# Gates computed with tokens on partitions, and the gated residual moved from GpSimd to VectorE

## The chip, the cores and the metric

One Trainium2 chip; the kernel runs on one of its cores. The metric is device time of one execution in microseconds (us), lower is better. PE is TensorE (PEld its weight loads), DVE is VectorE, ACT is ScalarE, POOL is GpSimd and SP is SyncE, which here issues nearly all DMAs.

## The reference

Eight batches of 512 tokens with 512 features, in f32. First a gated cross attention (an mLSTM, 4 heads of 128), then a gated mixture of 8 experts, 2 per token:

```python
ig = einsum(gin, w_igate) + b_igate;  fg = einsum(gin, w_fgate) + b_fgate      # gin = [q, k, v], k = v = ctx
pcs = cumsum(log_sigmoid(fg))                                                  # over the tokens
log_D = pcs[i] - pcs[j] + ig[j]   (j <= i);  D = exp(log_D - rowmax(log_D))
C = (q k^T / sqrt(dh)) * D
h = (C / (max(|C.sum|, exp(-rowmax)) + eps)) v;   h = layernorm over the head * (1 + ln_weight)
x = x + tanh(g_xattn) * h
x = x + tanh(g_ffn) * moe(layernorm(x))      # top 2 of 8 experts, gelu(x W1 + b1) W2 + b2, 1075 places each
```

With pcs and g = ig - pcs, the row maximum of log_D is pcs[i] + running maximum of g up to i. So D[j, i] = exp(g[j] - runmax[i]), and exp(-rowmax) = exp(-(pcs + runmax)).

## The kernel before

**The phases.** A first part (0 to about 387 us of the trace) does the attention for the eight batches, then comes the routing, and from about 471 us to the end the experts. In the experts `first_layer` and `second_layer` (lines 800 and 813) keep PE busy.

**Slots.** The attention runs in slots. In slot b every engine does work of several batches: b (scores, decays, head sums), b+1 ("front": turning q and ctx, gates), b+2 ("ahead": its first layer norm), b-1 ("back": norm of the heads, residual, second layer norm) and b-2 ("last": turning xn, router products). The order on each engine is written out in its `slot` function; there is no scheduler. An engine does its instructions strictly in that order, and semaphores make it wait. Slots 1 to 5 have all this work (slots 2 to 5 as a loop); slot 0 has no back, slot 6 no ahead, slot 7 neither ahead nor front, and the last batch's back work follows after slot 7.

**Gates.** `gate_products` (L651) multiplies the gate weights (36 columns, of which rows 0 to 3 and 32 to 35 of the result are the forget and input gates) with qT and kT: 8 matmuls of 512 columns, the result with gates on partitions, 4x512. DVE's `gates_first` (L1072 to L1075) adds the biases, ACT's `softplus` (L852, L853) follows, and `gates_second` (L1080 to L1089) does the log, a running sum (scan), g, a running maximum (scan), the negated maximum, and copies into `g_rows`. PE turns `g_rows` to columns (`gate_columns`, L658), DVE copies them (L1096). SP stores the negated maximum to memory (`spread_negmax`, L419) and loads it back spread over all partitions (L422). ACT makes the decays of a head from it (`exponentials`, L867), POOL masks them (`mask`, L531), and DVE multiplies them with the scores (`weigh`, L1104). PE makes the scores (L666) and the head sums (`outputs`, L675), ACT copies each head (`copy_head`, L873).

**Residual.** `back_stats` (L1117 to L1135) and `back_norm` (L1144) on DVE normalise the heads of batch b-1 with 16 operations of 128 columns. Then `residual` runs on POOL between mask 1 and mask 2: 4 products with gvec (ln_weight and tanh of the gate) into xn (L325) and 4 sums into x_back (L331), 512 columns each. For the last batch it runs on DVE. `row_stats` (L1046 to L1053) and `normalise` (L1056) are DVE's layer norms; `newton` (L1038 to L1041) refines the root that ACT seeds (L840, L841). SP loads x_back (L413), after it has issued the store of the previous xn (L431), the loads of ctx (L408) and of x_front (L401).

After the last slot POOL splits expert weights (`first_rests`, L556, L558), once ACT has cast them (L961, L962).

## Time and profile before

| | |
|---|---|
| three runs, us | 2086.21, 2086.83, 2087.01 (median 2086.83) |
| span of the profiled execution, first to last instruction, us | 2081.7 |
| what lies around the span, against the median, us | 5.1 |
| busy over the span: PE, DVE, ACT, POOL, us | 1928.8, 836.9, 713.2, 357.9 |
| busy in a slot of 44.20 us (175.60 to 219.80): PE, DVE, ACT, POOL, us | 38.06, 40.09, 18.69, 12.41 |

The shares of the whole span are those of the experts above all. The slots are read from the timeline of one slot, engine by engine. The times of the profiled execution stand for all: they come from one execution whose span is 5.1 us under the median of the timed runs, and a difference found in the span is taken as a difference of the time.

### The profile page before, as it was taken

The page shows a single profiled execution, that of the slowest core. Times are in us where ns is not written, and L with a number is a line of the kernel's source. Part 1 is how long each engine was busy: PE and PEld are TensorE (multiplying, and loading weights), DVE is VectorE, ACT ScalarE, POOL GpSimd, SP SyncE. Part 2 cuts the span into 40 slices and gives each one's busy share as a digit, 9 for nine tenths or more (in the row PEclk, how much of TensorE's full clock was granted, in tenths as well). Part 3 has the DMA queues.
Part 4 walks back from the last instruction along what each step waited for, and adds up shares of the span by engine and source line. Part 5 has one row for each costly group of instructions (what it writes and reads, how often), then busy time and mean ns, then how long its engine had stood idle before and what let it go on. Part 6 is the DMA issues. An engine that isn't in the chain of part 4 may idle for free.

```text
span 2081.7 us, 28147 instructions
## 1 busy us (share of the span) xinstructions
PE 1928.8 (93%) x10037; PEld 1636.3 (79%) x10037; DVE 836.9 (40%) x1879; ACT 713.2 (34%) x1447; POOL 357.9 (17%) x296
## 2 busy tenths in 40 slices
PE   5888888249999999999999999999999999999996
PEld 3555555148888888888888888888888888888885
DVE  4898987771224223512342143214322422242121
ACT  3444443312235223422442243224322532352221
POOL 1222233552100111011101111101110111001100
PEclk9999999679999999999999999999999999999998
DMA  4334532611104212411340133014310431041111
GB/s 139 102 122 154 164 128 102 201 61 55 29 10 141 75 29 50 139 36 29 78 128 20 29 99 112 20 25 118 107 22 10 138 84 29 14 137 34 29 15 14
DMA packets 104507, 157.53 MB, mean 76 GB/s; under 512 B 6912, under 2 KB 56192, under 8 KB 103376
## 3 DMA queue, kind: packets, MB, share of 16 engines
q1 hardware_dynamic: 88272, 120.54, 17.3%
q0 software_dynamic: 16128, 35.41, 9.4%
q8 instruction: 87, 1.43, 0.3%
q14 instruction: 20, 0.16, 0.0%
HBM read 120.85 MB, written 35.06 MB: 75 GB/s over the span
## 4 chain that ended last, share of the span: by engine, by line
PE 80%; DVE 13%; issue 2%; DMA 2%; ACT 1%; POOL 1%; DVEq 0%; POOLq 0%; ACTq 0%
PE PS L813 38%; PE PS L800 36%; DVE stats L1046 2%; PE PS L675 2%; PE PS L783 1%; DVE heads L1144 1%; DVE decay L1104 1%; DVE stats L1117 1%; PE PS L651 1%; DMA out_dram<-y_out,rows_add 1%; PE PS L666 1%; DVE g_max L1083 1%; DVE qn L1056 1%; DMA negmax<-negmax_rows 1%; DVE g_cum L1081 0%
## 5 line engine op out<-in xcount | busy, mean ns | idle before, releaser
L1312 DVE TENSOR_TENSOR h_lo<-h_raw,h_hi 128x360 fp32r<-128x360 f32 x384 | 205.1, 534 | 1081.8 <-ACT h_hi L1006 1076.1
L1005 ACT ACTIVATE h_raw<-PS,b_now 128x360 f32<-128x360 f32 x384 | 215.8, 562 | 1046.1 <-PE PS L800 1033.8
L800 PE MATMUL PS<-x_hi,w_hi 128*128 128x360 f32 x1536 | 504.1, 328 | 2.3 <-DVE x_lo L1299 1.3
L800 PE MATMUL PS<-x_hi,w_lo 128*128 128x360 f32 x1536 | 503.5, 328 | 0.0
L800 PE MATMUL PS<-x_lo,w_hi 128*128 128x360 f32 x1536 | 501.5, 326 | 0.0
L813 PE MATMUL PS<-w_hi,h_hi 128*120 128x512 f32 x1152 | 459.7, 399 | 0.0
L813 PE MATMUL PS<-w_lo,h_hi 128*120 128x512 f32 x1152 | 453.7, 394 | 0.0
L813 PE MATMUL PS<-w_hi,h_lo 128*120 128x512 f32 x1152 | 453.1, 393 | 0.0
L586 POOL DMA_INDIRECT out_dram<-y_out,rows_add x72 | 124.0, 1722 | 1341.9 <-DVE y_out L1340 1127.5
L800 PEld LDWEIGHTS PS<-x_hi,w_hi 128*128 128x128 f32 x1536 | 289.5, 188 | 24.2 <-issue 3.1
L800 PEld LDWEIGHTS PS<-x_lo,w_hi 128*128 128x128 f32 x1536 | 289.3, 188 | 16.4
L800 PEld LDWEIGHTS PS<-x_hi,w_lo 128*128 128x128 f32 x1536 | 289.9, 189 | 0.0
L813 PEld LDWEIGHTS PS<-w_hi,h_lo 128*120 128x120 f32 x1152 | 208.9, 181 | 59.1
L813 PEld LDWEIGHTS PS<-w_hi,h_hi 128*120 128x120 f32 x1152 | 209.1, 182 | 38.3
L813 PEld LDWEIGHTS PS<-w_lo,h_hi 128*120 128x120 f32 x1152 | 208.8, 181 | 38.2
L1006 ACT ACTIVATE h_hi<-PS,b_now 128x360 fp32r<-128x360 f32 x384 | 212.9, 554 | 0.0
L675 PE MATMUL PS<-vs,decay 128*128 128x129 f32 x640 | 87.3, 297 | 19.4 <-ACT heads L873 19.0
L675 PEld LDWEIGHTS PS<-vs,decay 128*128 128x128 f32 x640 | 84.8, 212 | 21.3 <-DVE decay L1104 14.9
L1292 DVE TENSOR_TENSOR w_lo<-raw,w_hi 128x512 fp32r<-128x512 f32 x112 | 77.5, 692 | 45.9 <-ACT w_hi L962 45.9
L666 PE MATMUL PS<-qT,kT 128*128 128x512 f32 (+3 forms) x256 | 82.6, 468 | 7.8 <-DVE decay L1104 7.8
L961 ACT CAST w_hi<-raw 128x512 fp32r<-128x512 f32 x128 | 79.8, 623 | 20.8 <-DMA raw<-in_L_ffn_W_dram 20.5
L666 PEld LDWEIGHTS PS<-qT,kT 128*128 128x128 f32 x256 | 44.3, 205 | 47.7 <-issue 20.5
(160 smaller groups left out, 1468.2 us busy)
## 6 DMA issues: line engine op xcount, KB each, us to landing
raw<-in_L_ffn_W_dram SPq DMA_DIRECT2D x128, 512.0 KB
x_front<-in_x_dram SPq DMA_DIRECT2D x8, 1024.0 KB, 7.0
vs<-in_ctx_dram SPq DMA_DIRECT2D x32, 256.0 KB, 4.6
negmax<-negmax_rows SPq DMA_DIRECT2D x8, 1024.0 KB, 4.7
x_back<-in_x_dram SPq DMA_DIRECT2D x8, 1024.0 KB, 8.9
out_dram<-x_back SPq DMA_DIRECT2D x8, 1024.0 KB, 4.4
xn_rows<-xn SPq DMA_DIRECT2D x8, 1024.0 KB, 5.2
b_row<-in_L_ffn_b_dram SPq DMA_DIRECT2D x8, 256.0 KB, 4.2
```

What stands on the lines that cost most here:

```text
L586: G.indirect_dma_start(out=out[:, :], out_offset=bass.IndirectOffsetOnAxis(ap=rows_add[u % CT][0:RT, :], axis=0), in_=y_out[0:RT, u % CT, ...
L651: ins = T.matmul(PS[0:GR, GATE, :], wgate[:, k, :], src, start=(k == 0), stop=(k == 2 * KT - 1))
L666: T.matmul(score_ps[t], kT[p][:, h, t * P:(t + 1) * P], qT[p][:, h, t * P:S], start=True, stop=True).then_inc(scores_made, 1)
L675: ins = T.matmul(head_ps[:, s, 0:DH + 1], decay[h % 2][:, t, s * P:(s + 1) * P], vs[p][:, t, h, 0:DH + 1], start=(t == 0), stop=(t == s))
L800: ins = T.matmul(PS[:, HB + n % 3, 0:CW], w[:, w_at(j), k * P:(k + 1) * P], v[:, c, k, :], start=(k == 0 and a == 0), stop=(k == KT - 1 an ...
L813: ins = T.matmul(PS[0:RT, YB + t, :], h[:, n % 3, t * RT:(t + 1) * RT], w[:, w_at(j), D:2 * D], start=(j == 0 and a == 0), stop=(j == HT - ...
L961: A.copy(w_hi[:, w_at(j), 0:D].rearrange("p (k c) -> p k c", k=KT), raw_w1(j))
L1005: A.activation(h_raw[:, n % 3, :], PS[:, HB + n % 3, 0:CW], ACT.Gelu, bias=b1_now[:, n % HT:n % HT + 1])
L1006: A.activation(h_hi[:, n % 3, :], PS[:, HB + n % 3, 0:CW], ACT.Gelu, bias=b1_now[:, n % HT:n % HT + 1]).then_inc(h_upper, 1)
L1046: ins = V.bn_stats(stats[kind][:, t, :], src[:, t, :])
L1292: V.tensor_tensor(w_lo[:, w_at(j), 0:D].rearrange("p (k c) -> p k c", k=KT), raw_w1(j), w_hi[:, w_at(j), 0:D].bitcast(F32).rearrange("p (k ...
L1312: V.tensor_tensor(h_lo[:, n % 3, :], h_raw[:, n % 3, :], h_hi[:, n % 3, :].bitcast(F32), ALU.subtract)\
```

## The change

Two parts, made together.

**Gates with tokens on partitions.** The gate weights shrink to 8 columns and become the moving operand; qT and kT are the weights. PE makes 32 products of 8 columns instead of 8 of 512, with the result [128 tokens, 4 tiles, 8 gates] (L634 of the changed kernel). Bias, absolute value, softplus and log then work on 128x32 and 128x16. The running sum is made by PE from a triangle of ones (`gate_sums`, 4 products). DVE takes g from it, PE turns g to rows (`turn_gates`), DVE makes the one scan that is left, the running maximum, from PSUM, PE turns the maxima to columns (`turn_maxima`), and DVE adds them to the sums (`gate_tops`). The maximum is stored as it is, and ACT negates it with its scale.

**Residual on VectorE.** The 16 operations of `back_norm` become (heads - mean) * gvec, and 16 more give x_back = heads * factor + x_back, 128 columns each. POOL has only the masks. The waits for back_turned and xn_stored, which POOL had, now stand before DVE's `second_norm`. DVE waits for the load of x_back right behind `weigh(b, 1)`.

```diff
-GR = 36
+GR = 2 * NH
...
-        gate_bias = sb("gate_bias", [GR, 1], F32, a_mem)
+        gate_bias = sb("gate_bias", [P, GR], F32, a_mem)
+        not_after = sb("not_after", [P, P], F32, a_mem)
...
-        def residual(engine, ops, b):
-
-            wait_apart(engine, heads_normed, at(b, 1, 1))
-            wait_apart(engine, back_turned, START + at(b, 4, 0))
-            wait_apart(engine, xn_stored, at(b, 16, 16))
-            for t in range(ST):
-                ins = ops.tensor_tensor(xn[:, t, :].rearrange("p (h c) -> p h c", h=NH), heads[b[1] % 2][:, t, :, 0:DH],
-                                        gvec[:, :].rearrange("p (h c) -> p h c", h=NH), ALU.mult)
-            ins.then_inc(heads_weighed, 1)
-            wait_apart(engine, x_back_in, at(b, 16, 16))
-            wait_apart(engine, heads_weighed, at(b, 1, 1))
-            for t in range(ST):
-                ins = ops.tensor_tensor(x_back[:, t, :], x_back[:, t, :], xn[:, t, :], ALU.add)
-            ins.then_inc(x1_made, 1)
-
...
-                wait_past(pe, gates_taken, at(b, 1, 0))
+                wait_past(pe, top_made, at(b, 1, 0))
                 if b[1] >= 2:
                     pe.wait_ge(back_copied, START + at(b, 4, -8))
-                for k in range(2 * KT):
-                    src = qT[p][:, k, :] if k < KT else kT[p][:, k - KT, :]
-                    ins = T.matmul(PS[0:GR, GATE, :], wgate[:, k, :], src, start=(k == 0), stop=(k == 2 * KT - 1))
+                for t in range(ST):
+                    for k in range(2 * KT):
+                        src = (qT[p] if k < KT else kT[p])[:, k % KT, t * P:(t + 1) * P]
+                        ins = T.matmul(gates_ps[:, t, :], src, wgate[:, k, :], start=(k == 0), stop=(k == 2 * KT - 1))
                 ins.then_inc(gates_made, 1)
 
-            def gate_columns(b):
-                wait_apart(pe, gate_rows_made, at(b, 1, 1))
-                wait_apart(pe, cols_copied, at(b, 1, 0))
+            def gate_sums(b):
+
+                pe.wait_ge(logs_made, at(b, 1, 1))
+                T.matmul(sums_ps, not_after[:, :], g_log[:, :, :], start=True, stop=False)
+                for t in range(ST - 1):
+                    earlier = g_log[:, t:t + 1, :].to_broadcast([P, ST - 1 - t, NH])
+                    ins = T.matmul(sums_ps[:, t + 1:ST, :], ones[:, 0:P], earlier, start=False, stop=(t == ST - 2))
+                ins.then_inc(sums_made, 1)
+
+            def turn_gates(b):
+
+                pe.wait_ge(cols_made, at(b, 1, 1))
                 for t in range(ST):
-                    ins = T.transpose(cols_ps[:, t, :], g_rows[:, t * P:(t + 1) * P], ident[0:GR, 0:GR])
-                ins.then_inc(cols_made, 1)
+                    ins = T.transpose(PS[0:NH, GATE, t * P:(t + 1) * P], cols[b[1] % 2][:, t, :], ident[:, :])
+                ins.then_inc(rows_made, 1)
+
+            def turn_maxima(b):
+
+                wait_apart(pe, max_made, at(b, 1, 1))
+                for t in range(ST):
+                    ins = T.transpose(max_ps[:, t, :], g_max[:, t * P:(t + 1) * P], ident[0:NH, 0:NH])
+                ins.then_inc(max_turned, 1)
...
                     gate_products(front)
                 if there(b):
                     scores(b, 2)
+                if there(front):
+                    gate_sums(front)
+                if there(b):
                     outputs(b, 1)
+                if there(front):
+                    turn_gates(front)
                 if there(last) and there(b):
                     router_products(last)
                 if there(b):
...
-                    gate_columns(front)
+                    turn_maxima(front)
...
-                    mask(b, 0)
-                    mask(b, 1)
-                if there(near(b, -1)):
-                    residual(pool, G, near(b, -1))
-                if there(b):
-                    mask(b, 2)
-                    mask(b, 3)
+                    for h in range(NH):
+                        mask(b, h)
 
...
-                gates = PS[:, GATE, :]
-                V.tensor_scalar(g_f[:, :], gates[0:NH, :], gate_bias[0:NH, 0:1], None, ALU.add)
-                chain(V.tensor_scalar(g_i[:, :], gates[32:32 + NH, :], gate_bias[32:32 + NH, 0:1], None, ALU.add))
-                dve.sem_inc(gates_taken, 1)
-                V.scalar_tensor_tensor(g_t[:, :], g_f[:, :], -1.0, g_f[:, :], ALU.mult, ALU.max).then_inc(abs_made, 1)
-
-            def gates_second(b, chain):
+                bias = gate_bias[:, :].rearrange("p (o g) -> p o g", o=1).to_broadcast([P, ST, GR])
+                chain(V.tensor_tensor(g_pre[:, :, :], gates_ps, bias, ALU.add))
+                f = g_pre[:, :, 0:NH]
+                V.scalar_tensor_tensor(g_t[:, :, :], f, -1.0, f, ALU.mult, ALU.max).then_inc(abs_made, 1)
+
+            def gate_logs(b):
                 dve.wait_ge(softplus_made, at(b, 1, 1))
-
-                chain(V.scalar_tensor_tensor(g_f[:, :], g_f[:, :], 0.0, g_t[:, :], ALU.min, ALU.subtract))
-                chain(V.tensor_tensor_scan(g_cum[:, :], ones[0:NH, :], g_f[:, :], 0.0, ALU.mult, ALU.add))
-                chain(V.tensor_tensor(g_i[:, :], g_i[:, :], g_cum[:, :], ALU.subtract))
-                chain(V.tensor_tensor_scan(g_max[:, :], ones[0:NH, :], g_i[:, :], LOWEST, ALU.mult, ALU.max))
-                wait_past(dve, negrow_out, at(b, 16, 0))
-                wait_past(dve, cols_made, at(b, 1, 0))
-                V.tensor_scalar(g_neg[:, :], g_max[:, :], -1.0, None, ALU.mult).then_inc(negrow_made, 1)
-                V.tensor_copy(g_rows[0:NH, :], g_i[:, :])
-
-                V.scalar_tensor_tensor(g_rows[32:32 + NH, :], g_cum[:, :], -1.0, g_max[:, :], ALU.mult, ALU.subtract)\
-                    .then_inc(gate_rows_made, 1)
+                V.scalar_tensor_tensor(g_log[:, :, :], g_pre[:, :, 0:NH], 0.0, g_t[:, :, :], ALU.min, ALU.subtract)\
+                    .then_inc(logs_made, 1)
 
             def gate_columns(b):
+                dve.wait_ge(sums_made, at(b, 1, 1))
+                wait_past(dve, decay_made, at(b, 4, -4))
+                V.tensor_copy(g_cum[:, :, :], sums_ps)
+                V.tensor_tensor(cols[b[1] % 2][:, :, :], g_pre[:, :, NH:GR], sums_ps, ALU.subtract).then_inc(cols_made, 1)
+
+            def gate_maxima(b):
+                dve.wait_ge(rows_made, at(b, 1, 1))
+                wait_past(dve, max_out, at(b, 16, 0))
+                V.tensor_tensor_scan(g_max[:, :], ones[0:NH, :], PS[0:NH, GATE, :], LOWEST, ALU.mult, ALU.max).then_inc(max_made, 1)
+
+            def gate_tops(b):
+                dve.wait_ge(max_turned, at(b, 1, 1))
                 dve.wait_ge(cols_made, at(b, 1, 1))
-                wait_past(dve, decay_made, at(b, 4, -4))
                 wait_past(dve, expneg_made, at(b, 1, -1))
-                V.tensor_copy(cols[b[1] % 2][:, :, :], cols_ps).then_inc(cols_copied, 1)
+                V.tensor_tensor(top_log[b[1] % 2][:, :, :], g_cum[:, :, :], max_ps, ALU.add).then_inc(top_made, 1)
 
             def weigh(b, h):
 
@@ -1141,9 +1145,20 @@
                 for t in range(ST):
                     for h in range(NH):
                         k = t * NH + h
-                        ins = V.tensor_scalar(hs[:, t, h, 0:DH], hs[:, t, h, 0:DH], small[1][:, 6, k:k + 1], small[1][:, 9, k:k + 1],
-                                              ALU.subtract, ALU.mult)
-                ins.then_inc(heads_normed, 1)
+                        ins = V.scalar_tensor_tensor(hs[:, t, h, 0:DH], hs[:, t, h, 0:DH], small[1][:, 6, k:k + 1],
+                                                     gvec[:, h * DH:(h + 1) * DH], ALU.subtract, ALU.mult)
+                chain(ins)
+
+            def residual(b):
+
+                hs = heads[b[1] % 2]
+                dve.wait_ge(x_back_in, at(b, 16, 16))
+                for t in range(ST):
+                    for h in range(NH):
+                        k = t * NH + h
+                        mine = x_back[:, t, h * DH:(h + 1) * DH]
+                        ins = V.scalar_tensor_tensor(mine, hs[:, t, h, 0:DH], small[1][:, 9, k:k + 1], mine, ALU.mult, ALU.add)
+                ins.then_inc(x1_made, 1)
 
             def second_stats(b, chain):
                 dve.wait_ge(x1_made, START + at(b, 1, 1))
@@ -1151,6 +1166,8 @@
 
             def second_norm(b, chain):
                 newton(2, b, ST, chain)
+                dve.wait_ge(back_turned, START + at(b, 4, 0))
+                dve.wait_ge(xn_stored, at(b, 16, 16))
                 for t in range(ST):
                     ins = normalise(2, t, xn, x_back)
                 ins.then_inc(xn_made, 1)
@@ -1170,21 +1187,28 @@
                     back_norm(back, chain)
                 if there(b):
                     weigh(b, 1)
+                if there(back):
+                    residual(back)
                 if there(ahead):
                     front_stats(ahead, chain)
+                if there(front):
+                    gates_first(front, chain)
+                if there(ahead):
                     front_norm(ahead, chain)
                 if there(front):
-                    gates_first(front, chain)
+                    gate_logs(front)
                 if there(b):
                     weigh(b, 2)
                 if there(front):
-                    gates_second(front, chain)
+                    gate_columns(front)
                 if there(back):
                     second_stats(back, chain)
+                if there(front):
+                    gate_maxima(front)
                 if there(b):
                     weigh(b, 3)
                 if there(front):
-                    gate_columns(front)
+                    gate_tops(front)
                 if there(back):
                     second_norm(back, chain)
...
-            residual(dve, V, LAST_BATCH)
+            residual(LAST_BATCH)
```

The order on PE in a slot, between the ctx turns and the last head sum: batch b's outputs 1, 2, 3 (L675, in the changed kernel L674) and scores 2, 3 (L666, now L665), with the front batch's gates between them. Before (slot 0, which has no router products):

```order
L651 MATMUL PS<-qT,wgate 36x512 x4
L651 MATMUL PS<-kT,wgate 36x512 x4
L666 MATMUL PS<-qT,kT 128x512
L666 MATMUL PS<-qT,kT 128x384
L666 MATMUL PS<-qT,kT 128x128
L666 MATMUL PS<-qT,kT 128x256
L675 MATMUL PS<-vs,decay 128x129 x10
```

and in the change:

```order
L634 MATMUL PS<-wgate,kT 128x8 x4
L665 MATMUL PS<-qT,kT 128x512
L665 MATMUL PS<-qT,kT 128x384
L665 MATMUL PS<-qT,kT 128x128
L665 MATMUL PS<-qT,kT 128x256
L640 MATMUL PS<-g_log,not_after 128x16
L643 MATMUL PS<-g_log,ones 128x12
L643 MATMUL PS<-g_log,ones 128x8
L643 MATMUL PS<-g_log,ones 128x4
L674 MATMUL PS<-vs,decay 128x129 x10
L650 MATMUL PS<-ident,cols 4x128 x4
```

Outputs 1 now stands behind the sums, which wait for DVE's log; the turn of g (L650) follows it, and the turn of the maxima (L657) takes the place that the turn of `g_rows` had, ahead of outputs 3.

The order on DVE in slot 1, from `weigh(b, 1)` on. Before:

```order
L1046 BN_STATS stats<-x_front 128x6 x4
L1051 BN_AGGR small<-stats 128x2 x4
L1053 TENSOR_SCALAR small<-small 128x4
L1038 TENSOR_TENSOR small<-small 128x4
L1039 TENSOR_TENSOR small<-small 128x4
L1040 TENSOR_SCALAR small<-small 128x4
L1041 TENSOR_TENSOR small<-small 128x4
L1056 TENSOR_SCALAR qn<-x_front,small 128x512 x4
L1072 TENSOR_SCALAR g_f<-PS,gate_bias 4x512
L1073 TENSOR_SCALAR g_i<-PS,gate_bias 4x512
L1075 SCALAR_TENSOR_TENSOR g_t<-g_f 4x512
```

and in the change:

```order
L1160 SCALAR_TENSOR_TENSOR x_back<-heads,small,x_back 128x128 x16
L1050 BN_STATS stats<-x_front 128x6 x4
L1055 BN_AGGR small<-stats 128x2 x4
L1057 TENSOR_SCALAR small<-small 128x4
L1076 TENSOR_TENSOR g_pre<-PS,gate_bias 128x32
L1078 SCALAR_TENSOR_TENSOR g_t<-g_pre 128x16
L1042 TENSOR_TENSOR small<-small 128x4
L1043 TENSOR_TENSOR small<-small 128x4
L1044 TENSOR_SCALAR small<-small 128x4
L1045 TENSOR_TENSOR small<-small 128x4
L1060 TENSOR_SCALAR qn<-x_front,small 128x512 x4
L1082 SCALAR_TENSOR_TENSOR g_log<-g_pre,g_t 128x16
```

The residual is ahead of the first layer norm, the gates' bias has moved ahead of `newton` and `normalise`, and only one small operation (L1082) is left between them and `weigh(b, 2)`.

## Rows read from the trace of the kernel before

**Rows 1.** The page: busy tenths in 40 equal slices of the span.

```profile
PE   5888888249999999999999999999999999999996
```

**Rows 2.** Busy time by stage: us, then busy (x instructions) of each engine, clock, DMA.

```profile
175.60:219.80 44.20, 38.06 (x193) 24.83 (x193) 40.09 (x114) 18.69 (x43) 12.41 (x12) 0.92 0.42 144
```

**Rows 3.** Timeline of DVE in slot 3: start, us, engine, line, operation, tiles [idle before].

```profile
175.52 1.67 DVE L1104 SCALAR_TENSOR_TENSOR decay<-PS,decay 128x512 f32<-128x512 f32 x4
...
180.12 0.55 DVE L1053 TENSOR_SCALAR small<-small 128x4 f32<-128x4 f32 x1
...
184.60 1.18 DVE L1041 TENSOR_TENSOR small<-small 128x4 f32<-128x4 f32 x1
...
187.91 0.73 DVE L1072 TENSOR_SCALAR g_f<-PS,gate_bias 4x512 f32<-4x512 f32 x1
...
190.27 1.69 DVE L1104 SCALAR_TENSOR_TENSOR decay<-PS,decay 128x512 f32<-128x512 f32 x4
...
203.37 0.16 DVE L1041 TENSOR_TENSOR small<-small 128x4 f32<-128x4 f32 x1
...
207.37 3.19 DVE L1117 BATCH_NORM_STATS2 stats<-heads 128x6 f32<-128x128 f32 x16 [1.78 <-ACT heads L873]
```

**Rows 4.** Timeline of POOL in slot 3, the sums of the residual.

```profile
180.83 4.92 POOL L331 TENSOR_TENSOR x_back<-x_back,xn 128x512 f32<-128x512 f32 x4 [0.18 <-POOL xn L325]
```

**Rows 5.** Timeline of PE in slot 3.

```profile
177.40 3.62 PE L651 MATMUL PS<-qT,wgate 128*36 128x512 f32 x8 [0.67 <-ACT kT L848]
...
184.39 2.42 PE L666 MATMUL PS<-qT,kT 128*128 128x512 f32 x8
186.65 2.40 PE L675 MATMUL PS<-vs,decay 128*128 128x129 f32 x20
188.98 3.60 PE L699 MATMUL PS<-xnT,wrouter 128*8 128x512 f32 x8
192.51 2.43 PE L666 MATMUL PS<-qT,kT 128*128 128x512 f32 x8
...
202.04 4.67 PE L675 MATMUL PS<-vs,decay 128*128 128x129 f32 x20 [3.63 <-ACT heads L873]
206.50 2.37 PE L666 MATMUL PS<-qT,kT 128*128 128x512 f32 x8
```

**Rows 6.** Stages of PE: us, PE busy (x), granted clock, DMA share, GB/s.

```profile
202.00:206.70 4.70, 4.66 (x21) 0.51 0.10 42
```

**Rows 7.** Instructions on DVE by form, 172 to 260 us: xcount | busy, mean ns.

```profile
L1144 DVE TENSOR_SCALAR heads<-heads,small 128x128 f32<-128x128 f32 x32 | 8.9, 350 | 0.1
```

**Rows 8.** Timeline of DVE and POOL behind the last slot.

```profile
373.07 4.20 DVE L1144 TENSOR_SCALAR heads<-heads,small 128x128 f32<-128x128 f32 x16
...
378.74 1.58 POOL L556 TENSOR_TENSOR w_lo<-raw,w_hi 128x512 fp32r<-128x512 f32 x1 [21.22 <-ACT w_hi L962]
...
380.97 6.57 DVE L331 TENSOR_TENSOR x_back<-x_back,xn 128x512 f32<-128x512 f32 x4
```

**Rows 9.** Timeline of PE's weight loads: 128 columns of weights for 8 moving ones.

```profile
197.09 0.32 PEld L706 LDWEIGHTS PS<-ident,logit_rows 8*128 8x128 f32 x4
```

**Rows 10.** The same at the start of the kernel.

```profile
11.45 0.49 PEld L623 LDWEIGHTS PS<-ident,rload 8*128 8x128 f32 x4
```

**Rows 11.** DMA: x_back's loads, 100 to 345 us.

```profile
DMA to landing us min/median/max: 7.6/8.9/9.3
```

**Rows 12.** Timeline of DVE, PE and SP at the start, the first gates.

```profile
29.34 0.74 DVE L1072 TENSOR_SCALAR g_f<-PS,gate_bias 4x512 f32<-4x512 f32 x1 [4.06 <-PE PS L651]
...
37.38 0.29 SPq L419 DMA_DIRECT2D negmax_rows<-g_neg  x1
```

**Rows 13.** Timeline of DVE in slots 6 and 7.

```profile
317.12 0.74 DVE L1072 TENSOR_SCALAR g_f<-PS,gate_bias 4x512 f32<-4x512 f32 x1 [7.34 <-PE PS L651]
...
356.97 1.69 DVE L1104 SCALAR_TENSOR_TENSOR decay<-PS,decay 128x512 f32<-128x512 f32 x4 [8.80 <-POOL decay L531]
```

**Rows 14.** Timeline of PE: a turn of q in slot 1, behind an idle stretch.

```profile
80.43 1.94 PE L639 MATMUL PS<-ident,qn 128*128 128x128 f32 x8 [2.74 <-ACT qT L848]
```

More of the change, by code:

```diff
@@ L163, in build @@
         decay = [sb(f"decay{p}", [P, ST, S], F32, a_mem) for p in range(2)]
-        negmax = [sb(f"negmax{p}", [P, NH, S], F32, a_mem) for p in range(2)]
+        maxima = [sb(f"maxima{p}", [P, NH, S], F32, a_mem) for p in range(2)]
         a_mem.close()
@@ L862, in exponentials @@
                 if h == 0:
-                    act.wait_ge(cols_copied, at(b, 1, 1))
-                    act.wait_ge(negmax_in[p], at_own(b, 16, 16))
+                    act.wait_ge(cols_made, at(b, 1, 1))
+                    act.wait_ge(maxima_in[p], at_own(b, 16, 16))
                 wait_past(act, head_summed, at(b, 4, h - 1))
                 for t in range(ST):
-                    ins = A.activation(decay[h % 2][:, t, t * P:S], negmax[p][:, h, t * P:S], ACT.Exp,
-                                       bias=cols[p][:, t, h:h + 1])
+                    ins = A.activation(decay[h % 2][:, t, t * P:S], maxima[p][:, h, t * P:S], ACT.Exp,
+                                       bias=cols[p][:, t, h:h + 1], scale=-1.0)
                 ins.then_inc(decay_made, 1)
```

71 lines of the change are left out of this document (36 added, 35 removed).

## The prediction

> **What bounds the kernel now.** I read the page first: PE is at nine tenths and more from the tenth of the 40 slices to the end [rows 1], and those are the experts, which the change does not touch. What it can move lies in the first 387 us. The busy time of a slot comes next: of 44.20 us DVE is busy for 40.09 and PE for 38.06 [rows 2], so both are near the limit and neither alone explains the slot. The timelines of the two tell it. DVE has two stretches with nothing idle, and one wait of 1.78 us, for ACT's copy of the last head [rows 3]. PE waits 3.63 us before the last head sum, and does it afterwards in 4.67 us where the same 20 instructions took 2.40 [rows 5]; the granted clock of that stretch is 0.51, the lower of the two levels (1.2 GHz), and it had been idle before [rows 6]. So the slot is a chain: DVE from the copied heads to `weigh(b, 2)`, then DVE's gates and second layer norm, then PE's last head sum.
>
> One more thing is to be seen in DVE's rows: an operation on 4 columns takes 0.16 us at 203.37, but 1.18 at 184.60 [rows 3], and those at 180 to 186 us lie under POOL's four sums, each about 1.23 us long [rows 4]. Each small operation waits for one of POOL's. The five of them take 5.7 us (180.12 to 185.78) instead of about 1.4 with the seed of ACT between.
>
> **The change, by parts.** The sum is made against the profiled execution (span 2081.7 us); the median of the three runs is 5.1 us above that, and I take every difference over unchanged.
>
> *A 128-column operation with a pointer scalar.* 16 of them take 4.20 us where nothing else runs [rows 8], 0.26 each, but those read one tensor. The new ones read two tensors and one pointer. The trace has no such form. From below, 16 operations of the same width without pointers take 3.19 us, 0.20 each (at 207.37) [rows 3]; from above, one of the old form lasts 0.35 us [rows 7], which is the cost if none overlaps with the next. I take 0.26, the nearest row: the heads' 16 cost what they did, and the 16 new ones 4.2 us (3.2 to 5.6). The Trainium skill (VectorE: DVE Perf Modes, the section on the TRN2 errata) says that a VectorE operation from SBUF pays 58 cycles beside its columns, and advises against small tiles. By it a new operation would be 186 cycles, 0.19 us, an estimate from the page, and the slots would be about 2 us shorter still; no row here has the form.
>
> *A slot, followed through slot 3.* DVE ends `weigh(b, 1)` at 177.2 [rows 3]. Residual: 4.2, and 0.5 for one mask of POOL that may fall into it, 181.9. Stats of the first layer norm, 3.1 as before, 185.0. The gates' first two operations, on 32 and 16 columns, 0.45, during which ACT makes the seed. `newton` 0.9 (four of 0.16 and their steps), `normalise` 2.0 (185.8 to 187.9), the log 0.2: 188.5. Before, `weigh(b, 2)` began at 190.27. So 4.2 of residual is paid for by 4.3 of waiting behind POOL and by the gates' bias, and DVE gains 1.8 us here.
>
> PE starts the gate products at 177.4 [rows 5]. They were 16 instructions in 7.0 us, and are 64, each with 128 weight columns and 8 moving ones. Four weight loads of that kind took 0.32 us, 0.08 each, at full clock [rows 9], and 0.49, 0.12 each, at the start [rows 10]. So the products cost 5.1 to 7.8; I take 6.5, between. They end at 183.9, before DVE asks at 185.0, and scores 2 at 186.2. The Trainium skill (TensorE: Matmul & The Clock Gate, section LDWEIGHTS) gives a weight load columns / 1.2 ns, 107 ns for 128 columns; by that it would be 6.8 us, an estimate from the page, again inside the cover that DVE gives.
>
> Now PE waits for the log: the new wait. At 188.6 the sums, 8 instructions, 0.7; behind them outputs 1 (2.3), the turn of g (0.4), router (3.5), scores 3 (2.3), outputs 2 (2.3), the turns of logits and maxima (0.7), outputs 3 (2.3), all from [rows 5]: 203.1. Before, outputs 3 ended at 206.5. DVE's scan waits for the turned g (192.0) and has 1.5 us of work; `weigh(b, 3)` waits for scores 3, and neither is late for outputs 3. The maxima are stored about when they were. A warm slot is 3.4 us shorter. Against it stands the clock: PE is idle for 2.4 us before the sums, with only thin products ahead of that. After 2.74 us of idling in slot 1, eight turns took 1.94 us [rows 14], not the usual 1.0. If outputs 1 ran at the lower level it would cost 2.3; I take 0.8 for it. **Five full slots at -2.6: -13.**
>
> *Start.* From the first gates to the store of the maximum it is 8.0 us (29.34 to 37.38) [rows 12]. The new path is 0.5 of bias and absolute value, 0.5 of softplus, 0.2 log, 0.9 sums, 0.4 columns, 0.6 turn, 1.3 scan, and 0.5 of steps between: 4.9. The weight copies shrink by 0.4. Together -3.5 (-5.5 to -1, by the price of the products). The first slot has no residual and waits for the load of the maxima; I put it at 0.
>
> *Slot 6.* DVE waits 7.34 us for the gates [rows 13]: here PE is the bound and the residual is free. PE gets the sums and a turn, 1.2 more, gates 0.5 less, and 0.8 for the clock: +1.5.
>
> *Slot 7.* DVE waits 8.80 us for a mask that stands behind POOL's residual [rows 13]. That goes; the next to be late is PE, whose router products lie ahead of scores 3. -2.5.
>
> *The last batch.* Its residual ran on DVE already, 377.27 to 387.54, 10.3 us, while POOL splits weights from 378.74 on [rows 8]; the 512-column sums went one for one with POOL's, 1.64 each. The new ones are 16, not 8, and smaller. Before POOL starts five are done. If the rest too go one for one, eight of them take 1.4 each (POOL has 8 operations ready, for four tiles), the last three 0.26: 13.3. So +2.8 (-4, if they do not alternate, to +5).
>
> *POOL, SP and ACT.* What POOL loses, 4.9 us of sums [rows 4] and nearly as much of products, was off the chain in all slots but slot 7. SP's order is unchanged. The load of x_back is issued behind the store of xn and the loads of ctx and x_front and takes 8.9 us [rows 11]; it lands about when the residual would start, and I give it nothing.
>
> Sum: -3.5 + 0 - 13 + 1.5 - 2.5 + 2.8 = -14.7, that is 2072 us.
>
> **The rivals.** *No fall of the clock.* Behind the gate products and scores 2, outputs 1 took 2.40 us before [rows 5], the time at full clock; if it stays so, the products at 0.08 take 5.1. Then a slot gains 3.4, five 17, slot 6 +(-0.8), the start -4.5, the rest as above: -22, 2065 us. Against it: PE now idles longer in that place than before.
>
> *The new operations do not overlap.* At 0.34 each 32 of them cost 2.6 more a slot, which takes the slots' whole gain; the last batch pays 1.3 more. -3.5 + 1.5 - 2.5 + 4.1 is -0.4: 2086 us. For it: two input tensors and a pointer, a form no row shows. Against: the other forms of that width all overlap.
>
> *Slower: the thin products let the clock fall, and it stays low to the end of outputs 1.* Place: PE from 177.4 on. Price: products 7.8, scores 2 4.6, sums 1.0, outputs 1 4.6, a turn 0.6: 196.1 instead of 192.0, so a slot is 0.7 us longer than before, five +3.7; slot 0 +4.5, slot 6, where PE is the bound, +6.9, start -2.5, slot 7 -2.5, last batch +2.8. Together +13, 2100 us. It decides once more than 3.3 us are lost ahead of the router products. For it: an instruction with 8 moving columns gives the array little work, and the clock fell behind 2.74 and 3.63 us of idling. Against: scores 2 are 2.3 us of dense work in between, and the wait is shorter than either.
>
> *The change does not free DVE.* If the slow small operations were not POOL's doing, 4.3 us would stay in each slot: log at 192.8, slots +1.6, in all +6, 2093 us. Against it stands that their ends fall on the ends of POOL's sums.
>
> **How the numbers follow.** Forecast 52 in 100, no fall of the clock 22, no overlap 13, slower by the clock 9, DVE not freed 4. The range reaches from 2059 (the second case with cheaper operations or a load of POOL that does not alternate) to 2087 (the third); the last two cases lie outside, and with the tails that is about 2 in 10. About 0.2% (4.2 us) is what a measurement of this kernel can tell from no change. Faster by more: 52 + 22 + 3 of the third case, 77; within: 10, the rest of the third; slower: 13.
>
> **What would show it.** In the changed profile a full slot should be 41 to 42 us, L1160 x16 about 4.2 us, L1042 to L1045 near 0.2 us each, L634 in 5 to 8 us, and PE idle for some 2 us before L640. The granted clock from the products to L674 tells the first rival and the slower one apart. Behind the last slot L1160 should alternate with POOL's L538 and L540. I am wrong if the slot is not shorter though DVE's small operations are fast again, or if DVE waits for the load of x_back.

## The result, and the profile after

The changed kernel is slower: 2111.16 us median of 4 runs (2110.62 to 2116.18) against 2086.52 us for the kernel before (4 runs, 2083.64 to 2087.01), a ratio of 1.0132 (1.0119 to 1.0145). The forecast was 2072, the range 2059 to 2087. The profiled execution took 2110.97 us with a span of 2109.2, which is 27.5 us more than the span of before. The medians are 24.6 us apart: in every run for which both are known 1.7 to 1.8 us lie around the span, so the profiled execution of before, with its 2081.7, must have taken about 2083.5, one of its fastest, and most of the 5.1 us that stand in the table of before are the difference between two executions. The stages below are laid out in spans, and are up to 3 us larger in sum than the medians would have them.

The page of the changed kernel, PE and its clock in 40 slices:

```profile
PE   5999999447999999999999999999999999999996
PEclk7778899769999999999999999999999999999998
```

In the slices that hold the batches, the first eight, PE is busier than in [rows 1], but at a granted clock of 0.7 to 0.9. Behind the batches the two kernels differ by 0.8 us in all (the last row of the table).

The loss can be laid out by stage if one operation is followed through both traces: the first instruction of `weigh(b, 1)` on DVE.

| stage | before, us | after, us | difference | forecast |
|---|---|---|---|---|
| start, to slot 0's `weigh(b, 1)` | 50.15 | 54.39 | +4.2 | -3.5 |
| slot 0 (to the same in slot 1) | 38.79 | 49.85 | +11.1 | 0 |
| slots 1 to 5, together | 219.17 | 225.12 | +6.0 | -13 |
| slot 6 | 38.39 | 44.09 | +5.7 | +1.5 |
| slot 7, to the last heads | 26.57 | 24.22 | -2.4 | -2.5 |
| last heads and last residual | 14.47 | 16.54 | +2.1 | +2.8 |
| the rest | | | +0.8 | |

The sum is +27.5. The last two forecasts hold; all four stages in which PE makes gate products are slower than forecast, by 4 to 19 us each. PE's timeline in slot 3 of the changed kernel shows why (start, duration; the new gate products are L634, in groups of eight instructions):

```profile
195.23 1.06 PE L634 MATMUL PS<-wgate,qT 128*128 128x8 f32 x8 [0.68 <-ACT kT L852]
196.15 1.04 PE L634 MATMUL PS<-wgate,kT 128*128 128x8 f32 x8
...
197.93 1.33 PE L634 MATMUL PS<-wgate,kT 128*128 128x8 f32 x8
199.11 1.85 PE L634 MATMUL PS<-wgate,qT 128*128 128x8 f32 x8
...
204.23 1.85 PE L634 MATMUL PS<-wgate,kT 128*128 128x8 f32 x8
205.94 3.80 PE L665 MATMUL PS<-qT,kT 128*128 128x512 f32 x8
209.57 0.29 PE L640 MATMUL PS<-g_log,not_after 128*128 128x16 f32 x2
...
210.38 2.48 PE L674 MATMUL PS<-vs,decay 128*128 128x129 f32 x20
```

A group of eight starts 0.90 us behind the one before, 0.112 us an instruction, until 197.93. From 199.11 on it is 1.71 us, 0.213 an instruction, and scores 2 (L665) take 3.63 us to the next start; they took 2.26 before [rows 5]. The 64 instructions take 10.7 us, not 6.5. Outputs 1 (L674) are back at 2.3 us. Windows of the same engine say what doubled (us, PE busy, granted clock, DMA share, GB/s); the first is slot 2's products, the next three are slot 3's products, scores 2, and what follows:

```profile
149.28:161.78 12.50, 12.50 (x65) 0.56 0.23 85
195.23:206.09 10.86, 10.86 (x65) 0.65 0.26 99
206.09:209.70 3.61, 3.61 (x10) 0.63 0.00 0
209.70:222.00 12.30, 12.30 (x77) 1.00 0.25 87
```

PE is busy for all of the products, yet the granted clock is 0.56 and 0.65: nearly all of one stretch and most of the other at the lower level, 1.2 GHz. Over the eight batches the products take 11.07, 12.60, 12.98, 12.51, 10.86, 10.36, 10.36 and 10.16 us, where the old ones took about 7.1 each.

DVE's timeline of the same slot:

```profile
193.81 1.69 DVE L1108 SCALAR_TENSOR_TENSOR decay<-PS,decay 128x512 f32<-128x512 f32 x4 [0.22 <-DVE heads L1148]
195.96 4.66 DVE L1160 SCALAR_TENSOR_TENSOR x_back<-heads,small,x_back 128x128 f32<-128x128 f32 x16 [0.47 <-DMA x_back<-in_x_dram]
...
206.12 0.19 DVE L1076 TENSOR_TENSOR g_pre<-PS,gate_bias 128x32 f32<-128x32 f32 x1 [2.37 <-PE PS L634]
...
207.05 0.16 DVE L1045 TENSOR_TENSOR small<-small 128x4 f32<-128x4 f32 x1
207.34 1.92 DVE L1060 TENSOR_SCALAR qn<-x_front,small 128x512 f32<-128x512 f32 x4
209.17 0.17 DVE L1082 SCALAR_TENSOR_TENSOR g_log<-g_pre,g_t 128x16 f32<-128x16 f32 x1
```

L1045 is back from 1.18 us to 0.16: DVE's small operations no longer wait for POOL [rows 3, 4]. DVE then waits 2.37 us for the gate products, which the forecast had under DVE's cover. Once the products are done, the log is made before PE asks for it: PE is not idle ahead of L640. Asked what waits for L634 in the whole kernel, the trace answers:

```profile
  DVE g_pre L1076: 48.9, 8
```

48.9 us in eight batches: 10.9 in the start and 14.1 in slot 0, where DVE has little else to do, and 1.9 to 6.0 in each of the six others. In the kernel before DVE waited 13.5 us for the gate products (L651), in three batches, and not at all in slots 1 to 5. The last batch went as forecast (heads, then the residual):

```profile
397.67 4.29 DVE L1148 SCALAR_TENSOR_TENSOR heads<-heads,small,gvec 128x128 f32<-128x128 f32 x16
401.99 12.22 DVE L1160 SCALAR_TENSOR_TENSOR x_back<-heads,small,x_back 128x128 f32<-128x128 f32 x16
```

### The profile page after: what moved, and what is told of

Same layout as the page of the kernel before. It is cut to its first block, busy times and chain, and to the rows that moved or that the text cites. A ratio compares the mean times of both kernels' runs of the same rounds, so it can differ in the third digit from the quotient of the medians.

```text
span 2109.2 us, 29090 instructions
## 1 busy us (share of the span) xinstructions
PE 1978.6 (94%) x10517; PEld 1721.5 (82%) x10517; DVE 802.4 (38%) x1967; ACT 708.1 (34%) x1447; POOL 289.6 (14%) x239
## 4 chain that ended last, share of the span: by engine, by line
PE 82%; DVE 7%; DMA 6%; issue 3%; ACT 1%; POOL 0%; POOLq 0%; DVEq 0%; ACTq 0%
PE PS L817 34%; PE PS L804 32%; DMA out_dram<-y_out,rows_add 5%; PE PS L634 4%; PE PS L674 3%; PE PS L665 3%; PE PS L787 1%; DVE stats L1121 1%; PE PS L698 1%; DMA gathered<-xn_rows,rows_turn 1%; PE PS L621 1%; DVE x_back L1160 1%; ACT kT L852 1%; ACT heads L877 0%; DVE heads L1148 0%
## 5 line engine op out<-in xcount | busy, mean ns | idle before, releaser
L665 PE MATMUL PS<-qT,kT 128*128 128x512 f32 (+3 forms) x256 | 95.4, 525 | 8.7 <-DVE decay L1108 8.7
L665 PEld LDWEIGHTS PS<-qT,kT 128*128 128x128 f32 x256 | 50.4, 231 | 48.2 <-issue 27.7
L965 ACT CAST w_hi<-raw 128x512 fp32r<-128x512 f32 x128 | 79.8, 624 | 18.5 <-DMA raw<-in_L_ffn_W_dram 18.2
L674 PE MATMUL PS<-vs,decay 128*128 128x129 f32 x640 | 79.7, 281 | 1.8 <-ACT heads L877 1.7
L966 ACT CAST w_hi<-raw 128x512 fp32r<-128x512 f32 x128 | 80.2, 627 | 0.0
```

The costliest lines, as they stand in the source:

```text
L665: T.matmul(score_ps[t], kT[p][:, h, t * P:(t + 1) * P], qT[p][:, h, t * P:S], start=True, stop=True).then_inc(scores_made, 1)
L674: ins = T.matmul(head_ps[:, s, 0:DH + 1], decay[h % 2][:, t, s * P:(s + 1) * P], vs[p][:, t, h, 0:DH + 1], start=(t == 0), stop=(t == s))
L965: A.copy(w_hi[:, w_at(j), 0:D].rearrange("p (k c) -> p k c", k=KT), raw_w1(j))
L966: A.copy(w_hi[:, w_at(j), D:2 * D], raw_w2(j)).then_inc(w_upper, 1)
```

## The experiments

Ten runs. Three theories of the loss stood against each other. **T1**: the clock, which the narrow products let fall. **T2**: DVE's added load or its new operations. **T3**: the new round trips between PE and DVE, where each waits for the other's result. The experiments compare with 7 to 19 runs of the kernel before on the same chip as each (medians 2084.1 to 2084.9 us).

### Each half of the change alone

`residual_only`: the kernel before with the residual on DVE and the weight of the heads folded into their normalising; the gates stay as they were.

```diff
-                if there(near(b, -1)):
-                    residual(pool, G, near(b, -1))
...
                     weigh(b, 1)
+                if there(back):
+                    residual(back)
```

> The kernel before with only the residual moved to VectorE (32 operations, GpSimd left with the masks), gates as before. Theory T1 (the gate products are the loss: 64 thin products at 0.11 us each, and 0.21 once the clock has fallen): this half is harmless or gains. DVE pays 4.3 to 4.7 us a slot and gets back 4.3 us of waits behind GpSimd, so a slot stays near 44 us; slot 7 gains about 2.5 us, the last batch loses about 2: 2080 to 2088 us. Theory T2 (VectorE's new load is the loss: the residual in its queue, the wait for x_back, and in the last batch the alternation with GpSimd): 2095 to 2105 us, with slots of 45 us and more.

Measured: 2086.35 us (10 runs), ratio 1.0006 (0.9996 to 1.0015). Its DVE timeline, in slot 3 and in the last batch:

```profile
178.73 4.66 DVE L1134 SCALAR_TENSOR_TENSOR x_back<-heads,small,x_back 128x128 f32<-128x128 f32 x16
...
187.60 0.16 DVE L1019 TENSOR_TENSOR small<-small 128x4 f32<-128x4 f32 x1
...
377.34 12.24 DVE L1134 SCALAR_TENSOR_TENSOR x_back<-heads,small,x_back 128x128 f32<-128x128 f32 x16
```

What DVE pays (4.66, and 0.15 more for the heads), it gets back from waiting behind POOL (about 4.3). The time is as T1 had it, and no different from before: this half is worth nothing, and T2 falls as a cause of the loss.

`gates_only`: the change with the residual put back on POOL.

```diff
-                    for h in range(NH):
-                        mask(b, h)
+                    mask(b, 0)
+                    mask(b, 1)
+                if there(near(b, -1)):
+                    residual(pool, G, near(b, -1))
```

> The changed kernel with the residual back on GpSimd, the gates with tokens on partitions kept. T1: the products take 10 to 12.6 us in every slot as in the full change and the kernel is 2105 to 2115 us. T2: most of the loss is gone, 2085 to 2092 us. If the new round trips between PE and VectorE (sums, turns) were the loss (T3), PE would wait 2 us and more ahead of the sums and of outputs 3, and the kernel would again be above 2105 us, but with the products near 7 us.

Measured: 2103.57 us, ratio 1.0109 (1.0077 to 1.0140), four executions of 2102.61 to 2115.47. The fifth, the profiled one, took 4514.53 us with all of PE's work stretched; why is open, and neither its time nor its trace is used here. The same kernel once more:

> The same kernel as the run of the gates part alone, for a profile of an ordinary execution. Products at 0.11 us each until the clock falls and 0.21 after it, 10 to 12.6 us in a slot, 2102 to 2106 us.

Measured: 2115.29 us (2103.06 to 2117.78, 4 runs), ratio 1.0130 (1.0099 to 1.0161), above what was expected in three of four executions. The trace has the same picture as the change, the fourth group of eight at 1.31 us and the next at 1.85:

```profile
203.65 1.31 PE L656 MATMUL PS<-wgate,kT 128*128 128x8 f32 x8
204.81 1.85 PE L656 MATMUL PS<-wgate,qT 128*128 128x8 f32 x8
```

So the gates half holds the loss by itself. The two measurements of one kernel differ by 12 us in their medians, far more than those of before. The other eight executions fall into two groups, and the mean granted clock goes with them: four took 2102.6 to 2103.6 us at 0.956 or 0.957, four took 2115.0 to 2117.8 at 0.949 to 0.951. So the time follows the clock here too; what puts an execution into one group or the other is open.

### The clock: the same instructions with wide products

`wide128`: the change, with the eight gate columns repeated sixteen times in `wgate`, so that each of the 64 instructions moves 128 columns and not 8. The other 120 columns of the result are read by nobody. The number of instructions, of weight loads, the order and the waits stay; four small copies are added at the start (1.25 us in the trace).

```diff
-        wgate = sb("wgate", [P, 2 * KT, GR], F32, a_mem)
+        wgate = sb("wgate", [P, 2 * KT, GW], F32, a_mem)
...
-                        ins = T.matmul(gates_ps[:, t, :], src, wgate[:, k, :], start=(k == 0), stop=(k == 2 * KT - 1))
+                        ins = T.matmul(wide_ps[:, t, :], src, wgate[:, k, :], start=(k == 0), stop=(k == 2 * KT - 1))
```

> The changed kernel, where each gate product multiplies 128 moving columns, the 8 gates repeated 16 times, of which 8 are used. As many products, as many weight loads, 16 times the columns. T1: the products are bound by their weight loads, so at full clock they stay at about 0.11 us each although they do 16 times the work, and because the array is then busy the clock does not fall: 64 take 7.2 us instead of 10.4 to 12.6, granted clock of the stretch 1.0, kernel 2080 to 2092 us (the copies of the gate columns at the start cost about 1.3 us). T2 and T3: nothing in their cause is changed, 2110 to 2114 us. If the clock falls whatever the columns, 64 products take 13 us, and the kernel is over 2115 us.

Measured: 2079.26 us (2074.34 to 2084.99, 10 runs), ratio 0.9974 (0.9964 to 0.9984), just under the 2080 of T1's range. That is sixteen times the multiplications, and 32 us less than the change. PE's timeline in slot 3:

```profile
177.89 1.16 PE L636 MATMUL PS<-wgate,qT 128*128 128x128 f32 x8 [0.67 <-ACT kT L854]
...
184.25 1.06 PE L636 MATMUL PS<-wgate,kT 128*128 128x128 f32 x8
185.14 2.32 PE L667 MATMUL PS<-qT,kT 128*128 128x512 f32 x8
189.88 0.40 PE L642 MATMUL PS<-g_log,not_after 128*128 128x16 f32 x2 [2.42 <-DVE g_log L1084]
...
190.80 2.48 PE L676 MATMUL PS<-vs,decay 128*128 128x129 f32 x20
```

and the windows of its products and of what follows the wait:

```profile
177.89:185.14 7.25, 7.25 (x65) 1.00 0.12 42
...
190.80:197.20 6.40, 6.40 (x35) 1.00 0.01 3
```

The products take 7.25 us, 0.112 us an instruction as the first ones of the change did, and the granted clock is 1.00. The wait for the log is there as predicted, 2.42 us, and outputs 1 behind it run at full clock. With the number of instructions and the waits in the program held, the clock is what is left as the cause of the change's loss: T1. Slots 1 to 5 take 42.6 us each (93.27 to 306.14), against 43.8 before and 45.0 in the change.

`wide_gates_only`: `wide128` with the residual back on POOL, the two edits above together.

> 128 moving columns a gate product, with the residual back on GpSimd: the gates part alone, with its clock mended. If the residual's move is neutral with these gates too, 2076 to 2082 us, equal to the 2079 us of the run with both. If the move pays once the gates are short (the small operations of VectorE then wait no longer behind GpSimd's sums on the chain), this one is slower than both by about 5 x 2 us, 2085 to 2090 us.

Measured: 2079.55 us (10 runs), ratio 0.9980 (0.9971 to 0.9990), the same as `wide128`. The residual's place changes nothing here either.

### Could the narrow products be had in another place?

`split_thin`: the change, with half of the gate products (token tiles 0 and 1) ahead of scores 2 and half behind.

```diff
-                    gate_products(front)
+                    gate_products(front, range(0, 2))
                 if there(b):
                     scores(b, 2)
                 if there(front):
+                    gate_products(front, range(2, ST))
+                if there(front):
                     gate_sums(front)
```

> The changed kernel with its 64 thin product instructions in two halves, token tiles 0 and 1 ahead of the scores of head 2, tiles 2 and 3 behind them. Columns, count and bytes as in the change. T1 (the clock falls because nothing but thin products runs for 7 us on end): each half lasts 3.6 us with dense work between, the granted clock stays up for all or most of it, the products take 7.2 us in sum and the kernel is near the one with 128 columns, 2080 to 2090 us. If thin products cost 0.21 us wherever they stand, the halves take 7 us each and the time stays at 2108 to 2113 us.

Measured: 2133.38 us (4 runs), ratio 1.0235 (1.0218 to 1.0252), the slowest of all, where T1 as I read it gave 2080 to 2090 and the other case no more than 2113: a miss. PE in slot 3:

```profile
205.22 1.38 PE L635 MATMUL PS<-wgate,kT 128*128 128x8 f32 x8
206.44 4.61 PE L667 MATMUL PS<-qT,kT 128*128 128x512 f32 x8
210.85 1.71 PE L635 MATMUL PS<-wgate,qT 128*128 128x8 f32 x8
...
220.99 0.61 PE L642 MATMUL PS<-g_log,not_after 128*128 128x16 f32 x2 [3.31 <-DVE g_log L1086]
...
222.72 4.16 PE L676 MATMUL PS<-vs,decay 128*128 128x129 f32 x20
```

with the clock of scores 2 and of the second half:

```profile
206.44:210.85 4.41, 4.41 (x9) 0.50 0.22 84
210.85:217.60 6.75, 6.75 (x33) 0.50 0.27 100
```

The clock falls in the fourth group of eight, as in the change. All of scores 2 then runs at 0.50, and so does the second half behind it; then comes a wait, and outputs 1 take 4.0 us, not 2.3. T1 stands; what I took from it, that a shorter stretch of narrow products escapes the fall, is wrong.

`thin_late`: the change with the sums moved behind outputs 1 and the turn of g behind the router, which gives DVE more time to make the log.

```diff
-                if there(front):
-                    gate_sums(front)
                 if there(b):
                     outputs(b, 1)
                 if there(front):
-                    turn_gates(front)
+                    gate_sums(front)
                 if there(last) and there(b):
                     router_products(last)
+                if there(front):
+                    turn_gates(front)
```

> The changed kernel with its 8-column products, and only the order of PE altered: the sums behind outputs 1, the turn of g behind the router products. With 128 columns this order gave 15 us. In the changed kernel PE had no idle time ahead of the sums, because the products at half clock end too late. If the fallen clock is what bounds the slot (T1), the order gives nothing or little: 2105 to 2112 us. If the new round trip between PE and VectorE was a loss of its own (T3), it gives its 2 us in five slots here too: 2096 to 2101 us.

Measured: 2117.23 us (2111.01 to 2118.74, 4 runs), ratio 1.0153 (1.0133 to 1.0173). That is above T1's 2105 to 2112 and far from T3's 2096 to 2101; against the change itself (1.0132, 1.0119 to 1.0145) it is not clearly slower. In slot 3 the fall comes in the second group of eight:

```profile
191.05 1.33 PE L634 MATMUL PS<-wgate,kT 128*128 128x8 f32 x8
192.23 1.85 PE L634 MATMUL PS<-wgate,qT 128*128 128x8 f32 x8
...
202.47 3.80 PE L665 MATMUL PS<-qT,kT 128*128 128x512 f32 x8
206.11 2.40 PE L674 MATMUL PS<-vs,decay 128*128 128x129 f32 x20
```

The granted clock is 0.57 from 190.13 to 206.11. With the products slow there is no wait for the log to be hidden, so the later order has nothing to give.

### Round trips, once the clock is kept

`wide_late`: the same order on top of `wide128`.

> 128 moving columns, and on PE the sums behind outputs 1, the turn of g behind the router products. In the run with 128 columns PE waited 2.42 us a slot for VectorE's log, ahead of the sums, with outputs 1 ready to run. If that wait is on the chain, outputs 1 fills it and each of the five full slots is 2.2 to 2.7 us shorter: 2066 to 2070 us. If VectorE or the load of x_back is what ends last, less than 1 us a slot: 2075 to 2079 us.

Measured: 2064.04 us (2061.20 to 2066.48, 4 runs), ratio 0.9903 (0.9886 to 0.9919), a little faster than the 2066 to 2070 expected if the wait was on the chain. PE in slot 3:

```profile
179.94 2.40 PE L676 MATMUL PS<-vs,decay 128*128 128x129 f32 x20
183.58 0.40 PE L642 MATMUL PS<-g_log,not_after 128*128 128x16 f32 x2 [1.25 <-DVE g_log L1084]
...
184.57 5.30 PE L700 MATMUL PS<-xnT,wrouter 128*8 128x512 f32 x8
```

The wait for the log is 1.25 us, not 2.42, and the turn of g waits for nothing. Slots 1 to 5 take 40.1 us each (90.41 to 290.90), 2.5 less than in `wide128`. So there is something in T3, 15 us by this order, but only here: the same edit on the narrow products gave nothing, and T3 is no cause of the change's loss. In this slot the router's products take 5.2 us instead of 3.5, at a granted clock of 0.67, which is more left to win; what lets the clock fall there was not tried.

### POOL in the last batch

`pool_waits`: the change, and POOL does not begin its splits of expert weights before the last residual is made.

```diff
+            pool.wait_ge(x1_made, START + B)
             first_rests(EARLY)
```

> The changed kernel, where GpSimd starts splitting expert weights only once the last batch's residual is done (a wait for x1_made). The 16 operations of the last residual took 12.22 us beside GpSimd's sums, 4.3 to 4.7 in the slots. If they alternate one for one with GpSimd's operations (T1 has this as a separate loss): they take 4.3 us, GpSimd has 12 us of idle time behind to catch up, and the kernel is 7 to 8 us faster, 2103 us. If GpSimd's later start delays the first expert weights instead, the time is unchanged or up to 5 us longer.

Measured: 2108.40 us (4 runs), ratio 1.0118 (1.0102 to 1.0135), 2.8 us under the change where 7 to 8 were expected, and within the spread of the two. DVE in the last batch:

```profile
398.18 4.29 DVE L1161 SCALAR_TENSOR_TENSOR x_back<-heads,small,x_back 128x128 f32<-128x128 f32 x16
...
407.53 1.19 DVE L1044 TENSOR_TENSOR small<-small 128x4 f32<-128x4 f32 x1
```

and POOL beside it:

```profile
407.44 1.25 POOL L538 TENSOR_TENSOR w_lo<-raw,w_hi 128x512 fp32r<-128x512 f32 x1
```

The residual falls from 12.22 to 4.29 us, and the small operations of the second layer norm then meet POOL instead, three of them one for one: 1.18 or 1.19 each where 0.16 is what they need. From the start of the last heads to the end of the last xn it is 20.2 us, and was 23.0 in the change: of 7.9 us gained in the residual about 5 are given back.

`wide_late_pool_back`: `wide_late`, POOL waits until the last batch's xn is made, and SP loads x_back ahead of x_front.

```diff
+                if there(back):
+                    load_back(back)
                 if there(ahead):
...
+            pool.wait_ge(xn_made, B)
             first_rests(EARLY)
```

> As the run with the sums behind outputs 1, and GpSimd starts the expert weights only when the last batch's xn is made, and SP issues the load of x_back ahead of that of x_front. The wait moves GpSimd past the last residual (12.2 to 4.3 us) and past the small operations and the normalise of the second layer norm, which in the run with the wait on the residual alone took 4.4 us longer beside GpSimd: 5 to 8 us are gained if GpSimd catches up later. The load of x_back was waited for in every second slot, 0.5 us each: 1 to 2 us. Together 7 to 10 us under the run without these two, 2057 to 2062 us if that is at 2068.

Measured: 2063.38 us (2061.17 to 2064.20, 4 runs), ratio 0.9902 (0.9885 to 0.9918): not to be told from `wide_late`, where 7 to 10 us less were expected: a miss, for the two edits together. Its last residual is free of POOL,

```profile
357.89 4.29 DVE L1164 SCALAR_TENSOR_TENSOR x_back<-heads,small,x_back 128x128 f32<-128x128 f32 x16
```

but from the last heads to the experts' first matmul it is still 97.2 us (353.56 to 450.79) against 98.65 in `wide_late`. Where the other 6.5 of the 7.9 us went was not followed up. These two are the fastest kernels of the study, 1% under the kernel before.

## Why the prediction was wrong, point by point

**The price of the gate products.** This is the step that failed: "So the products cost 5.1 to 7.8; I take 6.5, between." They took 10.2 to 13.0. A small part of the miss is the form. At full clock an instruction costs 0.112 us, 7.2 us for 64, which lies inside those bounds. But the rows under the value I took are of another form: in [rows 9, 10] the weights have 8 rows (`8*128`), in the products 128. Rows with full weights were at hand, eight turns of q in slot 3 of the kernel before:

```profile
208.71 1.04 PE L639 MATMUL PS<-ident,qn 128*128 128x128 f32 x8
209.58 0.60 PE L691 MATMUL PS<-ident,xn 128*128 128x128 f32 x4
```

The next group starts 0.87 us behind them, 0.109 us an instruction, which gives 7.0 us for 64. The Trainium skill (TensorE: Matmul & The Clock Gate, section LDWEIGHTS) gives the time of a weight load as its columns / 1.2 ns, 107 ns for 128 of them. The trace agrees with that to 5 ns as long as the clock is full; at the lower level it is 213 ns.

**The clock in the products.** The larger part, 3.5 of the 4.2 us in slot 3. I asked whether the clock would fall in the wait behind the products, and priced the products themselves at full clock even in the slower rival (the granted clock over [rows 10], from which the 7.8 comes, is 1.00). It fell inside them, with PE busy all the time, and each of the remaining instructions then took 0.213 us. That makes 10.2 to 13.0 us a batch, up to 5.2 above the upper bound, and scores 2 pays 1.4 more in slot 3. The old form, 16 instructions of 512 moving columns, had kept the clock at the same busy share: 6.99 us of 6.99 at 1.00 in slot 3. The slower rival had the right mechanism and place, at 9 in 100; its priced products were too cheap (7.8) and its outputs 1 too dear (4.6 forecast, 2.3 measured in slot 3, though 4.0 in slot 0), and it came to 2100.

**"They end at 183.9, before DVE asks at 185.0".** DVE's side of this is right to 1 us, as `wide128` shows best: there `weigh(b, 1)` starts at 176.46, 0.94 later than before; moved by that, the walk puts the log at 189.4, and it ended at 189.83. With narrow products the cover of 1.1 us turns into a wait of 2.37.

**Slot 0, the start and slot 6.** "I put it at 0", -3.5 and +1.5 came out at +11.1, +4.2 and +5.7. In these stages DVE waits for PE, 14.1, 10.9 and 6.0 us for the gate products, so what the products lose lands on the end. I treated them as edges of the sum; together they are 21 of the 27.5 us. In slot 0 the way from the start of the products to that of scores 3 took 22.8 us, not 11.5: the products 5.5 more, scores 2 2.1 more, outputs 1 1.7 more, and 2.0 for the new sums and the turn of g. The rows of the changed kernel for scores 2 and outputs 1:

```profile
73.06 4.61 PE L665 MATMUL PS<-qT,kT 128*128 128x512 f32 x8
...
79.03 4.13 PE L674 MATMUL PS<-vs,decay 128*128 128x129 f32 x20
```

`wide128` has +2.1 (of which 1.25 are its four copies), +2.3 and +0.8 there: even with the clock kept the gates half does not gain in them. For the start the trace of the change shows a term that the walk of 4.9 us left out. In DVE's new order `newton` and `normalise` stand between the gates' absolute value and the log, and there nothing else covers them:

```profile
33.58 1.92 DVE L1060 TENSOR_SCALAR qn<-x_front,small 128x512 f32<-128x512 f32 x4
35.41 0.17 DVE L1082 SCALAR_TENSOR_TENSOR g_log<-g_pre,g_t 128x16 f32<-128x16 f32 x1
```

ACT had ended the softplus at 33.36, so the log is 2.0 us late, and from the first gates to the store of the maximum it is 7.7 us (6.9 in `wide128`), where 8.0 was the time before. No run tried another order there.

**Full slots.** -2.6 each was forecast and +1.2 measured, and with it the first sign of being wrong that I had named: a slot that is not shorter though DVE's small operations are fast again. With the clock kept it is -1.3 on average and -1.0 in slot 3 (`wide128`). PE's outputs 3 ended 28.6 us behind the start of `weigh(b, 1)` in that slot, 27.6 was the forecast, and DVE's statistics of the heads began 1.1 us after the copy that they read. Among the five slots this gap stands only between slots 3 and 4, in the change too, and its row names no releaser but `issue`; that is where DVE's loop over pairs of slots turns round. In the kernel before, DVE had waited 1.78 us at that place for the copy [rows 3], which may have covered it. That the turn of the loop is the cause is not shown.

**The new operations.** "I take 0.26": 16 took 4.29 to 4.67 us, 0.27 to 0.29 each, so they overlap, and the rival without overlap falls. By the estimate from the Trainium skill (VectorE: DVE Perf Modes, the section on the TRN2 errata), 0.19 each, it would have been 3.1 us for 16; the measurement decides against it for this form.

**DVE freed.** Right: the small operations are back at 0.16 to 0.17 us. The sign "if DVE waits for the load of x_back" did come, but small: 0.47 us in slot 3, 0.16 and 0.49 in two other slots. But freeing DVE of those waits paid for the residual and no more, as the walk said (4.2 paid for by 4.3) and `residual_only` measured.

**Slot 7 and the last batch.** Right: -2.4 for -2.5, and the last residual took 12.22 us for 13.3, far above the 4.29 that `pool_waits` shows without POOL beside it, as foreseen.

## What to carry to other kernels

A reshaping that cuts a product into many instructions with few moving columns has to be priced at both clock levels: a PE that is busy without a gap is no sign that the clock holds, and the work behind it pays too. If the narrow form is wanted for its layout, filling the moving side with columns that nobody reads can cost nothing and keep the clock; here that was 32 us. A later place in PE's order for the work that waits for DVE gave 15 us once the clock had been kept, and nothing before; so the largest term is to be settled first. A later POOL gave 2.8 us at most in the one case and nothing that could be told in the other.

## What the runs showed of the hardware that I had not expected

- With 8 moving columns an instruction PE starts one each 0.112 us, and with 128 moving columns as well: in this shape the moving columns are free, and what sets the pace is something that both share.
- The granted clock went to its lower level while PE was busy for 100% of the stretch (0.56 over 12.50 us), and stayed at 1.00 in the same stretch of instructions with 128 columns. The place of the fall moved from batch to batch and from run to run: in the change it is the second group of eight in slots 0 to 2, the fourth in the start and in slot 3, and the fifth in slots 4 to 6, and in slot 3 of `thin_late` the second.
- At the lower level the start of one narrow instruction to the next took 0.213 us instead of 0.112, and so did that of their weight loads: eight in 1.71 us, not 0.90.
- Dense work behind the fall does not bring the clock back at once: in `split_thin` scores 2 ran for 4.41 us at 0.50, and the products behind them still ran at 0.50. In slot 3 of the change the clock was back before scores 2 had ended (0.63 over 3.61 us), in slot 0 not (4.41 us from their start to the next).
